# Attention: sums ahead of query halves, scaled diagonals on ScalarE, mask in the maximum

## The chip, the cores and the metric

The kernel runs on one core of a Trainium2 chip. The metric is the device time of one execution in microseconds. A core has five engines with a queue each, joined by semaphores: TensorE (PE; PEld is its weight load), VectorE (DVE), ScalarE (ACT), GpSimd (POOL) and SyncE (SP), which only issues transfers here. An engine takes its queue in order.

## The reference, cut to what matters

The kernel computes two transformer layers: linear attention and a mixture of experts, then causal attention and a feed-forward layer. The change touches the causal attention alone, here with B = 2 sequences of 1024 tokens and 16 heads:

```
qs  = concat([q_nope, rope(q_pe)])           # (b, h, s, 192), q = x @ wq
ks_ = concat([k_nope, rope(k_pe)])           # from a latent of 64
scores = einsum('bhqd,bhkd->bhqk', qs, ks_) * scale
scores = where(causal, scores, finfo.min)
attn = softmax(scores, axis=-1)
out = einsum('bhqk,bhkd->bhqd', attn, v)
```

## The kernel before

`phase_attention` runs once for each sequence. It goes through eight pairs of heads (`n`), and through ten steps (`x`) in each pair: a step is a block of 256 queries (`i`, 0 to 3) against a block of 256 keys (`jj` up to `i`). The steps that end a query block are x = 0, 2, 5 and 9 (`last_of`). The order on each engine is written out by hand, step by step.

**PE**, in step u: the score products of step u + 2 in two halves (`scores`, L1359, into one of two PSUM pairs), between and behind them what `aside` lists, then the value products of step u (`values`, L1382, into the bank `pv_ps`). `aside` lists in steps 0 to 3 one of the four query products of the next pair (`query`, L1327, all into the one bank `q_ps`), and in nearly all steps some pieces (`piece`, L1340): products of 128 queries with up to 512 keys, of which only the maximum of each row is wanted. There are 24 pieces to a pair, numbered 0 to 23, in two PSUM banks; 16 of them hold the causal diagonal, and for these a second matmul (L1343) adds -1e30 above it. In a middle pair steps 0 and 1 hold the pair's own last pieces, 21 to 23; steps 2 to 9 hold pieces 0 to 20 of the next pair. The maxima are subtracted from the scores by a last matmul of `scores` (L1365) with the matrix `minus`, four 128x128 diagonals to a query block.

**VectorE** does the rotary products of a query (`rope`, L1547 twice and L1550), the maxima of the pieces (`peaks`, L1555), behind the last piece of a block the diagonals (`spread`: L1564 joins the two halves of a row for blocks 2 and 3, L1568 writes the four diagonals), and reciprocals of the sums (`invert`, L1579). In steps 0 to 3 it takes the step's first piece ahead of the rotary products.

**ScalarE** does the exponentials (`probs`, L1441) and their rounding (`highs`, L1448) for step u + 2, in steps 0 to 3 the rounding of a query half (`q_high`, L1434, which waits for POOL's `rotate`), and at the end of a query block the copies of sums and products out of `pv_ps` (`sums`, L1459 and L1460). The first value product of the next block waits for them (`sums_sb`).

**POOL** completes the rotation (`rotate`, L1489), and computes the low halves of the queries (`q_low`, L1496), of the weights and of the exponentials (`low`, L1512), and the division's products (`product`, L1507).

A query thus goes: PE `query`, VectorE `rope`, POOL `rotate`, ScalarE `q_high`, POOL `q_low`; and since `q_ps` is one bank, query k + 1 waits for `rope` of query k.

## Time and profile before

| | us |
|---|---|
| median of three runs | 1459.39 (1458.5 to 1461.07) |
| the profiled execution | 1459.05 |
| its span, first to last instruction | 1457.2 |

| stretch, us | length | PE busy | DVE busy | ACT busy | POOL busy | granted clock |
|---|---|---|---|---|---|---|
| 500 to 890, attention of sequence 0 | 390 | 351.61 | 257.50 | 222.56 | 285.77 | 0.98 |
| 945 to 1333, attention of sequence 1 | 388 | 351.43 | 256.77 | 220.77 | 285.71 | 0.98 |
| the whole span | 1457.2 | 1227.6 | 844.7 | 626.2 | 961.9 | 0.93 |

The two attention stages are the same work twice. A matmul's record starts when it is issued and ends by a model of the pipeline, so neighbours overlap: the cost of one is read from the start of what follows. Where a row ends with a bracket, the engine was idle that long before it, and the name behind the arrow is what released it by the semaphores; where several semaphores are awaited, the view names the last to come by its inference, which can be another than the one that counted.

### The profile page before, as it was taken

The numbers are of one execution on the slowest core, as the hardware profiler recorded it, in microseconds if no ns is written. First come the engines' busy times: TensorE is split into PE (matmuls) and PEld (weight loads), VectorE is DVE, ScalarE is ACT, GpSimd is POOL, SyncE is SP. The second block draws the span as 40 slices with busy tenths as digits, with TensorE's granted clock in tenths as the row PEclk, the third lists the DMA queues.
The fourth block names the chain that finished last, engine by engine and source line by source line (L and its number), as shares of the span: only waits on it lengthen the run. The fifth ranks groups of instructions, "written<-read, shape, count | busy, mean of one in ns | idle before, by whom it ended". The sixth has DMA issues, their size and how long they took to land. (4 is left out here: it accounts for less than half of the span.)

```text
span 1457.2 us, 18876 instructions
## 1 busy us (share of the span) xinstructions
PE 1227.6 (84%) x5880; PEld 881.1 (60%) x5881; DVE 844.7 (58%) x1551; ACT 626.2 (43%) x1069; POOL 961.9 (66%) x700
## 2 busy tenths in 40 slices
PE   6974699999992489988998897689889998998797
PEld 5863455555551356666666666556666666666686
DVE  4578522222224667766676654767766776673567
ACT  3220233333320245565565564135655565565242
POOL 2025768888875457877788776557876787776454
PEclk9986799999995789999999998779999999999899
DMA  9348335555555000000000000000000000002001
GB/s 327 118 153 216 98 60 82 82 80 81 80 79 167 8 8 8 8 1 8 8 8 1 1 1 12 8 8 8 8 1 8 8 8 1 1 1 64 1 8 51
DMA packets 66509, 68.28 MB, mean 47 GB/s; under 512 B 15072, under 2 KB 59680, under 8 KB 66304
## 3 DMA queue, kind: packets, MB, share of 16 engines
q1 hardware_dynamic: 48336, 43.42, 10.0%
q0 software_dynamic: 15168, 20.72, 9.2%
q10 hardware_dynamic: 2928, 3.15, 0.7%
q8 instruction: 44, 0.72, 0.2%
q14 instruction: 33, 0.27, 0.1%
HBM read 46.17 MB, written 21.10 MB: 46 GB/s over the span
## 5 line engine op out<-in xcount | busy, mean ns | idle before, releaser
L1512 POOL TENSOR_TENSOR att_prob_lo<-att_prob,att_prob_hi 128x1024 fp32r<-128x1024 f32 (+1 forms) x160 | 346.7, 2167 | 114.1 <-ACT att_prob_hi L1448 114.0
L1555 DVE TENSOR_REDUCE att_peak<-all_bank 128x1 f32<-128x512 f32 (+3 forms) x384 | 207.4, 550 | 208.8 <-PE all_bank L1343 140.4
L1359 PE MATMUL all_bank<-att_q_hl,sequence_k_hl 128*128 128x512 f32 (+1 forms) x960 | 263.6, 385 | 0.0
L1382 PE MATMUL all_bank<-att_prob_hi,sequence_v_hl 128*128 128x512 f32 (+1 forms) x640 | 201.6, 396 | 35.3 <-POOL att_prob_lo L1512 19.1
L1441 ACT ACTIVATE att_prob<-all_bank 128x1024 f32<-128x1024 f32 (+1 forms) x160 | 150.6, 941 | 175.9 <-PE all_bank L1365 174.7
L1359 PEld LDWEIGHTS all_bank<-att_q_hl,sequence_k_hl 128*128 128x128 f32 x960 | 170.0, 192 | 26.1
L1340 PE MATMUL all_bank<-sequence_k_hl,att_q_hl 128*128 128x512 f32 (+3 forms) x384 | 171.0, 449 | 8.7 <-DVE att_peak L1555 8.3
L1448 ACT CAST att_prob_hi<-att_prob 128x1024 fp32r<-128x1024 f32 (+1 forms) x160 | 154.2, 964 | 5.1
L1327 PE MATMUL all_bank<-sequence_x_hl,sequence_w_hl 128*128 128x512 f32 x384 | 115.0, 438 | 46.3 <-DVE all_xT L1550 38.7
L1489 POOL TENSOR_TENSOR all_xT<-all_xT 128x512 f32<-128x512 f32 x64 | 82.4, 1288 | 106.1 <-DVE all_xT L1550 105.7
L916 PE MATMUL all_bank<-early_w_gu,moe_xgT 128*128 x316 | 148.9, 554 | 3.6 <-issue 2.4
L881 POOL DMA_INDIRECT sums<-moe_y,early_slot_far x79 | 125.5, 1589 | 36.0 <-issue 19.7
L1382 PEld LDWEIGHTS all_bank<-att_prob_hi,sequence_v_hl 128*128 128x128 f32 x640 | 108.0, 192 | 51.8 <-issue 24.7
L1579 DVE RECIPROCAL att_rden<-att_den 128x128 f32<-128x128 f32 x124 | 115.6, 939 | 26.8 <-POOL late_oT L1507 26.8
L1327 PEld LDWEIGHTS all_bank<-sequence_x_hl,sequence_w_hl 128*128 128x128 f32 x384 | 73.0, 201 | 77.2 <-DVE all_xT L1550 55.7
L1382 PE MATMUL all_bank<-att_prob_lo,sequence_v_hl 128*128 128x512 f32 x320 | 118.7, 371 | 0.0
L1365 PE MATMUL all_bank<-att_minus,all_bf 128*128 128x512 bf16 x320 | 117.6, 367 | 0.0
L1434 ACT CAST att_q_hl<-all_xT 128x512 fp32r<-128x512 f32 x64 | 39.7, 621 | 173.0 <-POOL all_xT L1489 173.0
L1008 DVE COPY moe_hidT<-all_bank 112x256 f32<-112x256 f32 x79 | 33.6, 425 | 123.4 <-PE all_bank L926 123.4
L1547 DVE TENSOR_TENSOR all_xT<-all_bank,sequence_cst_turned 32x512 f32<-32x512 f32 x128 | 88.8, 693 | 26.1 <-PE all_bank L1327 23.5
L871 POOL DMA_INDIRECT moe_xg<-x_rows,early_slot_row x79 | 84.2, 1065 | 26.1 <-issue 21.5
L935 PE MATMUL all_bank<-early_w_down,moe_hidT 112*128 x316 | 87.0, 398 | 12.1 <-issue 10.4
(244 smaller groups left out, 2103.6 us busy)
## 6 DMA issues: line engine op xcount, KB each, us to landing
sequence_w_raw<-wqk_rows SPq DMA_DIRECT2D x16, 256.0 KB, 2.7
early_w_gu<-in_gate SPq DMA_DIRECT2D x16, 224.0 KB, 5.7
early_w_gu<-in_up SPq DMA_DIRECT2D x16, 224.0 KB, 5.8
early_w_down<-in_down SPq DMA_DIRECT2D x1, 3584.0 KB, 19.8
sums<-early_zero SPq DMA_DIRECT2D x18, 128.0 KB, 3.7
all_xT<-in_xT SPq DMA_DIRECT2D x4, 512.0 KB, 7.6
all_x_tok<-in_x SPq DMA_DIRECT2D x1, 2048.0 KB, 16.3
x_rows<-all_x_tok SPq DMA_DIRECT2D x4, 512.0 KB, 3.0
```

The lines of the kernel that those rows point to most:

```text
L881: nc.gpsimd.indirect_dma_start(sums[s], bass.IndirectOffsetOnAxis(slot_far[:, r:r + 1], 0), y[:, s, :], None, bounds_check=last_far, compu ...
L916: mm = nc.tensor.matmul(gu_ps[s], xgT[:, s, k, :], w_gu[:, bass.ds(e * (KC * 2 * I) + k * 2 * I, 2 * I)], start=k == 0, stop=k == KC - 1)
L1327: mm = nc.tensor.matmul(q_ps, w_hl[:, ws, kc, h * P:(h + 1) * P], x_hl[:, xs, kc, c * WIDE:(c + 1) * WIDE], start=i == 0, stop=i == 3 * KC ...
L1340: mm = nc.tensor.matmul(ps[:, 0:w], q_hl[n % 2][:, 0, h, t * P:(t + 1) * P], k_hl[:, 0, k0:k0 + w], start=True, stop=not diagonal)
L1359: nc.tensor.matmul(ps, k_hl[:, ks, j * P:(j + 1) * P], q_hl[n % 2][:, qs, :, i * BW + q0:(i + 1) * BW], start=g == 0, stop=False)
L1365: mm = nc.tensor.matmul(ps, bf["ones"], minus[:, i, :].rearrange("p (h m) -> p h m", h=2)[:, :, q0:BW], start=False, stop=True)
L1382: mm = nc.tensor.matmul(out, v_hl[:, vs, j, :], part[:, u % 3, half * WIDE:half * WIDE + 2 * w].rearrange("p (h m) -> p h m", h=2), start= ...
L1441: nc.scalar.activation(prob[:, u % 2, 0:w], s_ps[u % 2][:, 0:w], ACT.Exp, scale=SCALE).then_inc(prob_sb, 1)
L1448: nc.scalar.copy(prob_hi[:, u % 3, 0:w], prob[:, u % 2, 0:w]).then_inc(hi_sb, 1)
L1512: nc.gpsimd.tensor_tensor(prob_lo[:, u % 3, 0:w], prob[:, u % 2, 0:w], prob_hi[:, u % 3, 0:w].bitcast(F32), ALU.subtract).then_inc(lo_sb, 1)
L1555: nc.vector.tensor_reduce(peak[:, n % 2, part, t // 2, h, t % 2:t % 2 + 1], piece_ps[y % 2][:, 0:w], AX_X, ALU.max).then_inc(peak_sb, 1)
L1579: nc.vector.reciprocal(rden[:, e % 2, cols], den[:, e % 2, cols]).then_inc(rden_sb, 1)
```

## The change

Four things in `phase_attention`, and the constants that they need.

- On ScalarE, `sums` stands ahead of `q_high` in a step. On POOL, `q_low` stands at the end of its own step, behind `low`, and no longer at the start of the next.
- The diagonals `minus` are made on ScalarE: `spread` is four activations of 128x128 (the identity, scaled by a row's maximum), at places given by `SPREAD_AT`: in step 4 for the next pair's block 0, in step 5 for block 1, in step 8 for block 2, in step 1 for the pair's own block 3. The sign moves into the stationary matrix (`less` holds -1).
- The matmul L1343 is gone. The maximum of a piece with the diagonal is one VectorE operation that adds the mask `late_wide` (in bf16; zeros, then the triangle), writes the sum back to the piece's bank and takes the maximum.
- The maximum of a row's second half starts from the first half's, so the join L1564 is gone.

```diff
@@ constants @@
-        bf = {n: bft[:, i, :] for i, n in enumerate(("ident", "ones", "late_q", "late_k"))}
+        bf = {n: bft[:, i, :] for i, n in enumerate(("ident", "less", "late_k"))}
+        bf["late_wide"] = bft[:, 4:8, :].rearrange("p a m -> p (a m)")
...
@@ the piece on PE @@
                     mm = nc.tensor.matmul(ps[:, 0:w], q_hl[n % 2][:, 0, h, t * P:(t + 1) * P],
-                                          k_hl[:, 0, k0:k0 + w], start=True, stop=not diagonal)
-                    if diagonal:
-                        mm = nc.tensor.matmul(ps[:, w - P:w], bf["late_q"], bf["ident"], start=False, stop=True)
+                                          k_hl[:, 0, k0:k0 + w], start=True, stop=True)
@@ ScalarE @@
+    SPREAD_AT = {4: [(1, 0)], 5: [(1, 1)], 8: [(1, 2)], 1: [(0, 3)]}
+                def spread(n, i):
+                    act.wait_ge(peak_sb, n * NP + block_needs[i])
+                    if n:
+                        act.wait_ge(s_mm, (n - 1) * NG + last_of[i] + 1)
+                    for a in range(4):
+                        done = nc.scalar.activation(minus[:, i, a * P:(a + 1) * P], bf["ident"], ACT.Copy,
+                                                    scale=peak[:, n % 2, 1, i, a // 2, a % 2:a % 2 + 1])
+                    done.then_inc(minus_sb, 1)
...
+                    if x in last_of:
+                        sums(n, last_of.index(x))
+                    for of, i in SPREAD_AT.get(x, ()):
+                        if 0 < n + of < PAIRS:
+                            spread(n + of, i)
+                    if n == 0 and x == 2:
+                        spread(0, NB - 1)
                     if made:
                         q_high(n + 1, x)
-                    if x in last_of:
-                        sums(n, last_of.index(x))
@@ POOL @@
-                        if 1 <= x <= QC:
-                            q_low(n + 1, x - 1)
...
+                    if n + 1 < PAIRS and x < QC:
+                        q_low(n + 1, x)
@@ VectorE @@
-                    nc.vector.tensor_reduce(peak[:, n % 2, part, t // 2, h, t % 2:t % 2 + 1], piece_ps[y % 2][:, 0:w],
-                                            AX_X, ALU.max).then_inc(peak_sb, 1)
-
-                def spread(n, i):
...
+                    half, whole = (peak[:, n % 2, a, t // 2, h, t % 2:t % 2 + 1] for a in range(2))
+                    if diagonal:
+                        if part:
+                            dve.wait_ge(peak_sb, n * NP + y - 1)
+                        nc.vector.tensor_tensor_reduce(ps, ps, bf["late_wide"][:, WIDE - w:WIDE], 1.0, half if part else MASKED,
+                                                       ALU.add, ALU.max, whole).then_inc(peak_sb, 1)
+                    else:
+                        nc.vector.tensor_reduce(half, ps, AX_X, ALU.max).then_inc(peak_sb, 1)
```

VectorE in steps 0 and 1 of a middle pair before (`all_xT` is the rotary's target, `att_peak` the maxima, `att_whole` and `att_minus` the join and the diagonals):

```order
L1550 TENSOR_TENSOR all_xT<-all_bank,sequence_cst_turned 128x512
L1555 TENSOR_REDUCE att_peak<-all_bank 128x1 x2
L1564 TENSOR_TENSOR att_whole<-att_peak 128x4
L1568 SCALAR_TENSOR_TENSOR att_minus<-all_bf,att_whole 128x512
L1547 TENSOR_TENSOR all_xT<-all_bank,sequence_cst_turned 32x512 x2
```

and now (each add-and-maximum is built as two ISA rows, the second of one column):

```order
L1567 TENSOR_TENSOR all_xT<-all_bank,sequence_cst_turned 128x512
L1577 ISA all_bank,att_peak<-all_bank,all_bf,att_peak 128x512
L1577 ISA att_peak 128x1
L1577 ISA all_bank,att_peak<-all_bank,all_bf,att_peak 128x512
L1577 ISA att_peak 128x1
L1564 TENSOR_TENSOR all_xT<-all_bank,sequence_cst_turned 32x512 x2
```

The join and the diagonals no longer stand between the last piece's maximum and the rotary products of the next query.

ScalarE in steps 0 and 1 of a middle pair before (`att_q_hl` is `q_high`, `att_den` and `late_oT` are the sums):

```order
L1448 CAST att_prob_hi<-att_prob 128x768
L1434 CAST att_q_hl<-all_xT 128x512
L1459 COPY att_den<-all_bank 64x256
L1460 COPY late_oT<-all_bank 64x256
L1459 COPY att_den<-all_bank 64x256
L1460 COPY late_oT<-all_bank 64x256
L1441 ACTIVATE att_prob<-all_bank 128x1024
L1448 CAST att_prob_hi<-att_prob 128x1024
L1434 CAST att_q_hl<-all_xT 128x512
```

and now:

```order
L1457 CAST att_prob_hi<-att_prob 128x768
L1468 COPY att_den<-all_bank 64x256
L1469 COPY late_oT<-all_bank 64x256
L1468 COPY att_den<-all_bank 64x256
L1469 COPY late_oT<-all_bank 64x256
L1433 CAST att_q_hl<-all_xT 128x512
L1450 ACTIVATE att_prob<-all_bank 128x1024
L1457 CAST att_prob_hi<-att_prob 128x1024
L1441 ACTIVATE att_minus<-all_bf,att_peak 128x128 x4
L1433 CAST att_q_hl<-all_xT 128x512
```

The sums have moved ahead of the query half, and four scaled copies stand in step 1 ahead of the next one.

## Rows read from the trace of the kernel before

**Rows 1.** busy us by stretch: length, PE, PEld, DVE, ACT, POOL, clock, DMA.

```profile
715.52:739.73 24.21, 20.18 (x97) 14.33 (x96) 15.05 (x24) 14.43 (x24) 17.60 (x12) 1.00 0.00 1
739.73:762.90 23.17, 23.15 (x118) 16.19 (x117) 17.61 (x28) 13.46 (x18) 18.48 (x12) 1.00 0.04 12
530.18:573.41 43.23, 40.21 (x197) 27.94 (x196) 34.81 (x52) 24.38 (x36) 32.90 (x21) 1.00 0.02 7
```

**Rows 2.** timeline, PE, one pair: start, us, instruction, [idle before <-releaser].

```profile
716.37 1.74 PE L1327 MATMUL all_bank<-sequence_x_hl,sequence_w_hl 128*128 128x512 f32 x6
...
721.85 1.65 PE L1327 MATMUL all_bank<-sequence_x_hl,sequence_w_hl 128*128 128x512 f32 x6 [0.58 <-DVE all_xT L1550]
...
725.55 0.70 PE L1382 MATMUL all_bank<-att_prob_hi,sequence_v_hl 128*128 128x512 f32 x2 [0.82 <-ACT late_oT L1460]
...
729.13 1.67 PE L1327 MATMUL all_bank<-sequence_x_hl,sequence_w_hl 128*128 128x512 f32 x6 [1.02 <-DVE all_xT L1550]
...
734.38 1.65 PE L1327 MATMUL all_bank<-sequence_x_hl,sequence_w_hl 128*128 128x512 f32 x6 [0.36 <-DVE all_xT L1550]
...
736.52 0.23 PE L1343 MATMUL all_bank<-all_bf 128*128 128x128 bf16 x1
738.02 0.71 PE L1382 MATMUL all_bank<-att_prob_hi,sequence_v_hl 128*128 128x512 f32 x2 [1.26 <-POOL att_prob_lo L1512]
...
763.78 1.74 PE L1327 MATMUL all_bank<-sequence_x_hl,sequence_w_hl 128*128 128x512 f32 x6
```

**Rows 3.** timeline, ScalarE of the same pair.

```profile
725.04 0.36 ACT L1460 COPY late_oT<-all_bank 64x256 f32<-64x256 f32 x1
...
737.51 0.36 ACT L1460 COPY late_oT<-all_bank 64x256 f32<-64x256 f32 x1
...
746.25 1.03 ACT L1441 ACTIVATE att_prob<-all_bank 128x1024 f32<-128x1024 f32 x1 [1.59 <-PE all_bank L1365]
```

**Rows 4.** timeline, VectorE of the same pair.

```profile
724.77 0.69 DVE L1555 TENSOR_REDUCE att_peak<-all_bank 128x1 f32<-128x512 f32 x1 [2.38 <-PE all_bank L1343]
725.50 0.71 DVE L1564 TENSOR_TENSOR att_whole<-att_peak 128x4 f32<-128x4 f32 x1
...
726.97 1.40 DVE L1547 TENSOR_TENSOR all_xT<-all_bank,sequence_cst_turned 32x512 f32<-32x512 f32 x2
...
738.52 0.69 DVE L1550 TENSOR_TENSOR all_xT<-all_bank,sequence_cst_turned 128x512 f32<-128x512 f32 x1
```

**Rows 5.** timeline, PE at two like spots, without and with L1343.

```profile
714.93 0.40 PE L1340 MATMUL all_bank<-sequence_k_hl,att_q_hl 128*128 128x512 f32 x1
...
715.40 0.28 PE L1382 MATMUL all_bank<-att_prob_lo,sequence_v_hl 128*128 128x256 f32 x1
...
719.46 0.40 PE L1340 MATMUL all_bank<-sequence_k_hl,att_q_hl 128*128 128x512 f32 x1
...
720.06 0.28 PE L1382 MATMUL all_bank<-att_prob_lo,sequence_v_hl 128*128 128x256 f32 x1
```

**Rows 6.** groups by shape, VectorE: busy us, mean ns | idle before.

```profile
L1555 DVE TENSOR_REDUCE att_peak<-all_bank 128x1 f32<-128x512 f32 x160 | 108.5, 688 | 116.8 <-PE all_bank L1340 62.3 <-PE all_bank L1343 52.3
...
L1929 DVE SCALAR_TENSOR_TENSOR ffn_hid<-all_bank,late_s_up,ffn_gated 128x512 f32<-128x512 f32 x20 | 14.9, 747 | 24.8 <-ACT ffn_gated L1886 15.4 <-POOL ffn_hid_hl L1903 9.2
...
L707 DVE TENSOR_TENSOR_SCAN route_ties_so_far<-route_ones,route_tie 128x256 f32<-128x256 f32 x1 | 0.7, 682 | 0.0
...
L806 DVE TENSOR_SCALAR route_far<-early_cst 128x1 f32<-128x1 f32 x1 | 0.1, 145 | 0.0
```

**Rows 7.** groups by shape, ScalarE.

```profile
L1886 ACT ACTIVATE ffn_gated<-all_bank,late_s_gate 128x512 f32<-128x512 f32 x20 | 13.8, 688 | 24.8 <-PE all_bank L1841 24.8
...
L649 ACT COPY early_z<-all_bank 128x128 f32<-128x128 f32 x16 | 3.5, 269 | 37.8 <-PE all_bank L608 37.8
```

**Rows 8.** timeline, step 8 of that pair, POOL, then PE.

```profile
752.73 2.39 POOL L1512 TENSOR_TENSOR att_prob_lo<-att_prob,att_prob_hi 128x1024 fp32r<-128x1024 f32 x1
...
757.57 0.62 PE L1382 MATMUL all_bank<-att_prob_hi,sequence_v_hl 128*128 128x512 f32 x2
```

More of the change, by code:

```diff
@@ L63, in const_columns @@
     for name, width in (("ident", P), ("cos", QT * ROPE), ("sin", QT * ROPE), ("before", P), ("iota", P), ("headmask", P),
-                        ("late_q", P), ("late_k", P), ("late_cols", 2 * P), ("row", 1)):
+                        ("late_q", P), ("late_k", P), ("late_cols", P), ("row", 1)):
         at[name] = (n, n + width)
@@ L96, in const_table @@
     put("late_k", np.where(f >= p, MASKED, 0.0))
-    q = np.arange(2 * P)[None, :] - P
-    put("late_cols", p == np.maximum(q + 1, 0))
+    put("late_cols", p == f + 1)
     put("row", p)
@@ L230, in _ @@
                 nc.gpsimd.memset(power[:], -0.5).then_inc(ones_sb, 1)
-                nc.gpsimd.memset(bf["ones"], 1.0)
+                nc.gpsimd.memset(bf["less"], -1.0)
                 pool.wait_ge(loaded_x, 32)
@@ L405, in _ @@
                 dve.wait_ge(loaded_cst, 32)
-                for name in ("ident", "late_q", "late_k", "late_cols"):
+                for name in ("ident", "late_k", "late_cols"):
                     nc.vector.tensor_copy(bf[name], cst[name])
+                nc.vector.memset(bf["late_wide"][:, 0:WIDE - P], 0.0)
+                nc.vector.tensor_copy(bf["late_wide"][:, WIDE - P:WIDE], cst["late_q"])
                 for n in range(B * KC):
@@ L1286, in phase_attention @@
         peak = m.sb("peak", [P, 2, 2, NB, 2, 2])
-        whole = m.sb("whole", [P, 2, NB, 2, 2])
         minus = m.sb("minus", [P, NB, WIDE], BF16)
@@ L1334, in piece @@
                     _, n, y = item
-                    t, h, _, k0, w, diagonal = pieces[y]
+                    t, h, _, k0, w, _ = pieces[y]
                     if n * NP + y >= 2:
@@ L1362, in scores @@
                         nc.tensor.matmul(ps[:, :, 0:P], bf["late_k"],
-                                         bf["late_cols"][:, P:2 * P].unsqueeze(1).to_broadcast([P, 2, P]),
+                                         bf["late_cols"].unsqueeze(1).to_broadcast([P, 2, P]),
                                          start=False, stop=False)
-                    mm = nc.tensor.matmul(ps, bf["ones"], minus[:, i, :].rearrange("p (h m) -> p h m", h=2)[:, :, q0:BW],
+                    mm = nc.tensor.matmul(ps, bf["less"], minus[:, i, :].rearrange("p (h m) -> p h m", h=2)[:, :, q0:BW],
                                           start=False, stop=True)
@@ L1464, in _ @@
                     q_high(0, k)
+                spread(0, 0)
+                spread(0, 1)
                 weights_high(1)
@@ L1467, in _ @@
                 highs(0)
+                spread(0, 2)
                 probs(1)
@@ L1552, in peaks @@
                 def peaks(n, y):
-                    t, h, part, _, w, _ = pieces[y]
+                    t, h, part, _, w, diagonal = pieces[y]
+                    half, whole = (peak[:, n % 2, a, t // 2, h, t % 2:t % 2 + 1] for a in range(2))
+                    ps = piece_ps[y % 2][:, 0:w]
                     dve.wait_ge(max_mm, n * NP + y + 1)
-                    nc.vector.tensor_reduce(peak[:, n % 2, part, t // 2, h, t % 2:t % 2 + 1], piece_ps[y % 2][:, 0:w],
-                                            AX_X, ALU.max).then_inc(peak_sb, 1)
-                def spread(n, i):
-                    top = peak[:, n % 2, 0, i]
-                    dve.wait_ge(peak_sb, n * NP + block_needs[i])
-                    if i >= NB // 2:
-                        top = whole[:, n % 2, i]
-                        nc.vector.tensor_tensor(top, peak[:, n % 2, 0, i], peak[:, n % 2, 1, i], ALU.max).then_inc(whole_sb, 1)
-                        dve.wait_ge(whole_sb, n * (NB // 2) + i - NB // 2 + 1)
-                    if n:
-                        dve.wait_ge(s_mm, (n - 1) * NG + last_of[i] + 1)
-                    nc.vector.scalar_tensor_tensor(minus[:, i, :].rearrange("p (a m) -> p a m", m=P),
-                                                   bf["ident"].unsqueeze(1).to_broadcast([P, 4, P]), -1.0,
-                                                   top.rearrange("p h t -> p (h t)").unsqueeze(2).to_broadcast([P, 4, P]),
-                                                   ALU.mult, ALU.mult).then_inc(minus_sb, 1)
+                    if diagonal:
[5 more added lines that the diff above has]
+                        nc.vector.tensor_reduce(half, ps, AX_X, ALU.max).then_inc(peak_sb, 1)
                 def invert(e, half):
@@ L1586, in beside @@
                         peaks(n, v)
-                        if v + 1 in block_needs:
-                            spread(n, block_needs.index(v + 1))
                 dve.wait_ge(turned_loaded, 16)
@@ L1948, in program @@
         cst = {n: cst_kept[:, a:z] for n, (a, z) in at.items() if z <= kept}
[L1949 to L1951 removed]
+        bft = m.sb("bf", [P, 8, P], BF16)
+        bf = {n: bft[:, i, :] for i, n in enumerate(("ident", "less", "late_k"))}
+        bf["late_cols"] = bft[:, 3:4, :].rearrange("p a m -> p (a m)")
+        bf["late_wide"] = bft[:, 4:8, :].rearrange("p a m -> p (a m)")
         power = m.sb("power", [P, NT])
```

6 lines of the change are left out of this document (2 added, 4 removed).

## Prediction

> **What bounds the kernel now.** I read the stage first, then the queues inside it. There are two attention stages, one per sequence, with eight head pairs each and ten steps to a pair. Pairs 1 to 6 repeat themselves: the query matmuls of one pair's step 0 start at 716.37 and those of the next at 763.78, 47.4 us later [rows 2]. So I take one pair apart and multiply by 12 (six in each sequence). 
>
> The waits of steps 1 to 3 are in the PE timeline [rows 2]. Three are queries waiting for the rotary product of the query before (0.58, 1.02 and 0.36 us), because one PSUM bank holds them all. Two are the first value product of a query block, at 725.55 (0.82) and 738.02 (1.26). Those wait for the sums of the block before. The ScalarE rows show it [rows 3]: the last copy of the sums ends at 725.04 + 0.36 = 725.40 and at 737.51 + 0.36 = 737.87, each 0.15 ahead of the matmul. The view names a POOL subtraction for the second; by the code that matmul needs only an earlier subtraction, so I put it to the copies. They are late because they stand behind `q_high`, which waits for POOL's rotation, though `pv_ps` was complete long before.
>
> **Part 1, sums ahead of `q_high`.** The four copies start as soon as `highs(u+2)` and the value products are done, some 3 us earlier in step 0 and 2 us in step 2. Both waits go. But what is late next is the rotary chain: query k+1 waits for VectorE's rotary of query k, which stands behind the maxima of a piece that PE issues after `scores(u+2, 1)`. A PE that reaches query 2 at 729.13 - 1.02 - 0.95 still needs the rotary to be done. So the step-1 wait is worth only what the chain gives back, which is part 2's business; the step-3 wait comes back in full, as nothing but `sums` and `low` holds the value product there. ScalarE now blocks on the value products in steps 0 and 2 ahead of `q_high`; `q_high` waits for the rotation anyway, which ends later. On POOL only a `product` in step 3 changes places with `q_low`, which nothing waits for.
>
> **Part 2, the diagonals leave VectorE.** In step 1 VectorE does the last piece's maximum (724.77), then `whole` (725.50) and the `minus` diagonals, and only then the rotary, at 726.97 [rows 4]. From 725.50 to 726.97 that is 1.47 us straight on the chain to query 2. Elsewhere the other three spreads stand where VectorE has room: nothing is gained.
>
> **Part 3, the mask moves from a matmul to the maximum.** The matmul L1343 (128 columns, 256 in all, 16 to a pair) costs its columns and a weight load that has nothing to hide behind. Two like spots show it [rows 5]: from a 512-wide piece to the start of the last of three 256-wide value matmuls it is 715.40 - 714.93 = 0.47 without it and 720.06 - 719.46 = 0.60 with it, so 0.13 us each.
> In its place 256 of the 384 maxima become an add-and-maximum that is two instructions: one over the columns that writes them back to PSUM, one that reads out a 128x1 result. The trace has no such pair, so I bound it [rows 6]. A 512-wide maximum is 688 ns and a two-input operation out of PSUM with a per-partition scalar 747; a 128x1 operation takes 145. Below nothing it can't be: the same columns pass, and an instruction is added. Low end 0 (the tail hidden), and at 512 columns high end 0.6, by the furthest row, the scan that carries a value from column to column: 682 ns for 256 columns, the rate of two passes. I take 0.16 (0.06 for the scalar, 0.10 of the tail), since a running maximum is what the reduction already does at full rate.
>
> **Part 4, the diagonals arrive on ScalarE.** Four 128x128 scaled copies to a spread. A 128x128 copy took 269 ns, a 128x512 activation with a per-partition scale 688, a quarter of it 172 [rows 7]; the 256-wide copies 360 [rows 3]. So 0.7 to 1.5 us a spread; I take 1.3, near the 128x128 row plus a pointer. That is 5.2 us a pair, on an engine busy 27.9 of 47.4 [rows 1]. The cover: step 1's runs while ScalarE would wait for the rotation, those of steps 4, 5 and 8 in gaps like the 1.59 us at 746.25 [rows 3]. The tightest place behind them is step 8's value product, whose subtraction ended at 752.73 + 2.39 = 755.12 with the matmul at 757.57 [rows 8], 2.45 us of margin. Two spreads (2.6) stand ahead of it on ScalarE, and PE comes sooner; the gaps swallow most, and I reckon 0.4 us left.
> A rule speaks against this part: the Trainium skill, ScalarE: Activation LUTs, Rules for kernel authors, says to do multiplications on VectorE, not ScalarE, VectorE being up to about three times faster. By the figures of that page of the Trainium skill (186 ns fixed, 93 for a pointer operand, 0.833 a column, neighbours overlapping by 93) a spread would be an estimated 1.2 us, against 0.69 for VectorE's one instruction. The rows agree on the price and not on the advice: ScalarE waits there, and VectorE holds the chain.
>
> **The sum for one pair**, step by step:
> - Query 2 before: 729.13. Less 0.13 (no L1343 ahead of the piece's maximum), plus 0.16, less 1.47: 727.69, a gain of 1.44. PE itself would be there about 727.05, so it still waits 0.6 for the rotary.
> - Query 3: again 0.13 less and 0.16 more: gain 1.41, at 732.97.
> - Step 3's value product: before, 738.02. Its piece and L1343 ended at 736.52 + 0.23 = 736.75, which is 2.37 after query 3; without the 0.13 it follows 2.24 after 732.97, at 735.21: gain 2.81. The copies it needs are done by about 734. With one more L1343 in that step, 2.94.
> - Steps 4 to 9: eleven L1343, 1.43. But VectorE's rotary of query 3 ended at 738.52 + 0.69, half a us ahead of step 4 [rows 4]; it now ends about 1.1 us behind its start, and the third piece of step 4 waits about 0.45 for a free bank. Left: 0.98.
> Together 3.9 us a pair, 47 us for twelve. The first pair of each sequence idles less (43.23 - 40.21 = 3.0 [rows 1]) and has the same 16 matmuls; I take 2.5 each, 5 in all. The last pair has two L1343: 0.5 for both. The opening ahead of the first pair loses three spreads on VectorE and pays sixteen maxima; I take 1 us each (0 to 2), 2 in all. The VectorE and POOL constants at the start cost nothing: VectorE waits for PE right after. Sum 54.5. The profiled run took 1459.05, so 1404.6; the median is 0.3 above it: **1405 us**.
>
> **Rivals.**
> *ScalarE becomes the bound.* If a scaled copy is 0.5 us rather than 0.33, a spread is 2.0, step 8's subtraction comes 1.4 later with 0.4 to spare: 1 us a pair lost in step 8 and about as much again in steps 4 to 6, where the sums stand behind a spread: 12 to 24 us back, 1417 to 1429. For it: an engine that goes from 59% to over 75% with queued waits. Against: the price would be past every row above. The rule of the Trainium skill named above points to this rival; its price is worked out from the rows.
> *The chain holds more than I think.* If PE merely waits elsewhere (pieces waiting for maxima in steps 4 to 9), the 1.43 of the matmuls does not come back and some of the 1.44 neither: 2 to 2.5 us a pair, 1425 to 1435. Against: VectorE was busy 17.6 of 23.2 in steps 4 to 9 and loses three spreads there.
> *Slower.* The add-and-maximum is so dear that VectorE sets steps 1 to 9. Two of them stand on the rotary chain and twelve behind it in steps 3 to 9, where VectorE has some 6 us free, about 0.5 each. Past 0.5 extra, every 0.1 costs 1.4 us a pair; the 3.9 are eaten at about 0.75 extra, and at 0.9 the kernel takes 1485. For it: it writes PSUM where the maximum wrote one column. Against: the two-input row of 747 ns runs at the rate of the reduction, and even the scan's rate would stay below 0.75.
> *Better than the sum.* Tail hidden, step 4 without a wait: 4.5 us a pair, about 1396.
>
> **How the numbers follow.** Forecast (1397 to 1414) 0.62; better 0.06; ScalarE bound 0.12; chain holds more 0.14; slower 0.03; and 0.03 for ending within 0.2%, about what a measurement can tell from no change. That gives faster 0.94, same 0.03, slower 0.03. The range leaves out the slow end and the farthest of the better: 1393 to 1428.
>
> **What would show it.** Right: a pair repeats at about 43.5 us; no wait of a value product on the sums in steps 1 and 3; queries 1 to 3 still waiting 0.5 to 0.8 us for the rotary; the 512-wide add-and-maximum with its tail at 0.8 to 0.9 us; four scaled copies in 1.3 us. Wrong: value products waiting for POOL's subtraction in steps 6 and 8 (ScalarE), or pieces waiting for maxima all through steps 4 to 9 (VectorE).

## The result

| | before | after |
|---|---|---|
| median, us | 1459.39 | 1401.61 (1399.83 to 1404.18, four runs) |
| profiled execution, us | 1459.05 | 1404.18 |
| its span, us | 1457.2 | 1402.4 |
| granted clock over the span | 0.93 | 0.93 |

The ratio is 0.9614, with an interval of 0.9596 to 0.9631: 57.8 us less. 1405 was predicted, in a range from 1393 to 1428. The profiled execution is the slowest of the four, so the spans differ by less than the medians.

Where the time went is told by the two attention stages, each taken from the first pair's first value products to the last pair's last. Together they took 718.15 us before and take 667.88 now: 50.3 of the 54.8 us by which the spans differ. The remaining 4.5 us lie in the rest of the program, where only the openings ahead of the first pairs and the constants changed. In the kernels below this rest varies from 728 to 739 us, so small edits are judged by the stages ("stages" in the table of experiments).

### The profile page after: what moved, and what is told of

It reads as the page before. It is cut to its first block and busy times, and to the rows that moved or that the text cites. A ratio compares the mean times of both kernels' runs of the same rounds, so it can differ in the third digit from the quotient of the medians.

```text
span 1402.4 us, 18855 instructions
## 1 busy us (share of the span) xinstructions
PE 1188.5 (85%) x5570; PEld 877.9 (63%) x5625; DVE 789.7 (56%) x1712; ACT 697.6 (50%) x1325; POOL 956.0 (68%) x700
## 5 line engine op out<-in xcount | busy, mean ns | idle before, releaser
L1358 PE MATMUL all_bank<-att_q_hl,sequence_k_hl 128*128 128x512 f32 (+1 forms) x960 | 257.1, 378 | 0.0
L1381 PE MATMUL all_bank<-att_prob_hi,sequence_v_hl 128*128 128x512 f32 (+1 forms) x640 | 190.4, 379 | 16.8 <-ACT late_oT L1469 15.3
L1328 PE MATMUL all_bank<-sequence_x_hl,sequence_w_hl 128*128 128x512 f32 x384 | 115.1, 438 | 48.1 <-DVE all_xT L1567 40.5
L1381 PEld LDWEIGHTS all_bank<-att_prob_hi,sequence_v_hl 128*128 128x128 f32 x640 | 112.7, 189 | 41.0 <-issue 22.1
L1580 DVE TENSOR_REDUCE att_peak<-all_bank 128x1 f32<-128x512 f32 (+1 forms) x128 | 83.7, 657 | 74.1 <-PE all_bank L1341 69.9
L1577 DVE CUSTOM_DVE_ANT_0 all_bank<-all_bank,all_bf,att_peak 128x256 f32<-128x256 f32 (+2 forms) x128 | 75.6, 591 | 75.9 <-PE all_bank L1341 73.9
L1564 DVE TENSOR_TENSOR all_xT<-all_bank,sequence_cst_turned 32x512 f32<-32x512 f32 x128 | 88.8, 693 | 26.4 <-PE all_bank L1328 23.8
L1577 DVE CUSTOM_DVE_ANT_0 all_bank<-all_bank,all_bf 128x128 f32<-128x128 f32 (+3 forms) x128 | 63.0, 499 | 60.9 <-PE all_bank L1341 60.3
```

The costliest lines, as they stand in the source:

```text
L1328: mm = nc.tensor.matmul(q_ps, w_hl[:, ws, kc, h * P:(h + 1) * P], x_hl[:, xs, kc, c * WIDE:(c + 1) * WIDE], start=i == 0, stop=i == 3 * KC ...
L1358: nc.tensor.matmul(ps, k_hl[:, ks, j * P:(j + 1) * P], q_hl[n % 2][:, qs, :, i * BW + q0:(i + 1) * BW], start=g == 0, stop=False)
L1381: mm = nc.tensor.matmul(out, v_hl[:, vs, j, :], part[:, u % 3, half * WIDE:half * WIDE + 2 * w].rearrange("p (h m) -> p h m", h=2), start= ...
L1564: nc.vector.tensor_tensor(swapped[o:o + 32, c % 2], q_ps[i:i + 32], sin[i:i + 32, cols], ALU.mult)
L1577: nc.vector.tensor_tensor_reduce(ps, ps, bf["late_wide"][:, WIDE - w:WIDE], 1.0, half if part else MASKED, ALU.add, ALU.max, whole).then_i ...
```

## The profile after

Stretches of one middle pair, steps 0 to 3 and steps 4 to 9, and of the first pair: length, then busy us of PE, PEld, DVE, ACT and POOL, granted clock, DMA share, GB/s. They answer [rows 1].

```profile
700.68:722.07 21.39, 19.03 (x92) 14.19 (x91) 12.74 (x23) 15.05 (x28) 16.22 (x11) 1.00 0.00 1
722.07:744.46 22.39, 21.86 (x106) 16.46 (x106) 16.88 (x39) 17.25 (x31) 19.50 (x13) 1.00 0.05 13
529.52:569.24 39.72, 37.25 (x177) 27.78 (x178) 29.17 (x64) 28.68 (x52) 32.30 (x21) 1.00 0.03 8
```

The clock is 1.00 in all three, as before. Steps 0 to 3 became 2.8 us shorter, steps 4 to 9 only 0.8, and in those TensorE now idles 0.53 us. The PE timeline of the pair shows each wait, as [rows 2] did:

```profile
701.65 1.74 PE L1328 MATMUL all_bank<-sequence_x_hl,sequence_w_hl 128*128 128x512 f32 x6
707.13 1.66 PE L1328 MATMUL all_bank<-sequence_x_hl,sequence_w_hl 128*128 128x512 f32 x6 [0.95 <-DVE all_xT L1567]
712.98 1.64 PE L1328 MATMUL all_bank<-sequence_x_hl,sequence_w_hl 128*128 128x512 f32 x6 [0.72 <-DVE all_xT L1567]
718.17 1.64 PE L1328 MATMUL all_bank<-sequence_x_hl,sequence_w_hl 128*128 128x512 f32 x6 [0.43 <-DVE all_xT L1567]
720.71 0.71 PE L1381 MATMUL all_bank<-att_prob_hi,sequence_v_hl 128*128 128x512 f32 x2 [0.26 <-ACT late_oT L1469]
732.38 0.69 PE L1381 MATMUL all_bank<-att_prob_hi,sequence_v_hl 128*128 128x512 f32 x2 [0.53 <-ACT late_oT L1469]
...
745.43 1.74 PE L1328 MATMUL all_bank<-sequence_x_hl,sequence_w_hl 128*128 128x512 f32 x6
```

From query 0 to query 0 it is 43.78 us (47.41 before). Three queries still wait for the rotary product. The 0.95 of the first holds a matmul whose record is missing, L1364 ahead of the query: in the six middle pairs that have the record the wait is 0.72, and the step is as long. Of the value products, step 1's no longer waits, step 3's waits 0.26 instead of 1.26, and step 6's waits 0.53 where the view of before has no bracket (what that hides is told under "L1343" below). ScalarE of the same pair shows why:

```profile
719.06 0.37 ACT L1468 COPY att_den<-all_bank 64x256 f32<-64x256 f32 x1 [1.40 <-DVE att_rden L1588]
...
720.20 0.36 ACT L1469 COPY late_oT<-all_bank 64x256 f32<-64x256 f32 x1
...
726.93 1.27 ACT L1441 ACTIVATE att_minus<-all_bf,att_peak 128x128 bf16<-128x128 bf16 x4
...
730.74 0.37 ACT L1468 COPY att_den<-all_bank 64x256 f32<-64x256 f32 x1
...
731.87 0.36 ACT L1469 COPY late_oT<-all_bank 64x256 f32<-64x256 f32 x1
732.26 1.28 ACT L1441 ACTIVATE att_minus<-all_bf,att_peak 128x128 bf16<-128x128 bf16 x4
```

In step 2 the sums, now ahead of `q_high`, wait 1.40 us for VectorE's reciprocals of the block two before, whose `den` buffer they take, and end at 720.56, 0.15 ahead of the value product. In step 5 they stand behind the scaled copies of step 4 and all that those pushed back, and end at 732.23, again 0.15 ahead of the value product.

VectorE on the chain to query 2 (compare [rows 4]), with no join and no diagonals between maximum and rotary:

```profile
709.97 0.76 DVE L1577 CUSTOM_DVE_ANT_0 all_bank<-all_bank,all_bf,att_peak 128x512 f32<-128x512 f32 x1 [2.17 <-PE all_bank L1341]
710.64 0.14 DVE L1577 DVE_READ_ACCUMULATOR2_ANT att_peak<- 128x1 f32 x1
710.82 1.40 DVE L1564 TENSOR_TENSOR all_xT<-all_bank,sequence_cst_turned 32x512 f32<-32x512 f32 x2
```

Groups by shape, busy us and mean ns of one, the new operations on ScalarE and VectorE (compare [rows 6, 7]):

```profile
L1441 ACT ACTIVATE att_minus<-all_bf,att_peak 128x128 bf16<-128x128 bf16 x256 | 81.6, 390 | 9.7 <-DVE att_peak L1577 9.4
...
L1577 DVE DVE_READ_ACCUMULATOR2_ANT att_peak<- 128x1 f32 x256 | 36.3, 142 | 0.0
...
L1577 DVE CUSTOM_DVE_ANT_0 all_bank<-all_bank,all_bf,att_peak 128x512 f32<-128x512 f32 x32 | 24.2, 755 | 33.6 <-PE all_bank L1341 33.3
L1577 DVE CUSTOM_DVE_ANT_0 all_bank<-all_bank,all_bf 128x512 f32<-128x512 f32 x32 | 22.3, 702 | 12.3 <-PE all_bank L1341 12.3
```

## Experiments

Steps are those of a middle pair, from the last value product of one to that of the next, in us; "pair" is the sum of all ten. A ratio is taken against runs of the kernel before made beside the kernel's own (p1 and p2 ran twice, the others four to ten times). What other steps do is told where it matters.

| kernel | median | ratio to before | stages | step 1 | 2 | 3 | 6 | pair |
|---|---|---|---|---|---|---|---|---|
| before | 1459.39 | | 718.15 | 6.74 | 5.90 | 6.81 | 3.99 | 47.4 |
| a1_sums | 1457.59 | 0.9984 [0.9959, 1.0009] | 719.82 | 5.73 | 8.46 | 5.73 | 4.01 | 47.9 |
| a2_diag | 1451.39 | 0.9952 [0.9932, 0.9972] | 710.93 | 6.72 | 5.13 | 6.81 | 3.99 | 46.6 |
| a3_mask | 1436.12 | 0.9859 [0.9826, 0.9891] | 695.30 | 6.84 | 5.61 | 6.75 | 4.00 | 45.8 |
| after | 1401.61 | 0.9614 [0.9596, 0.9631] | 667.88 | 5.72 | 5.49 | 5.65 | 4.30 | 43.8 |
| u1_sums_behind | 1417.91 | 0.9712 [0.9679, 0.9745] | 682.69 | 6.85 | 4.51 | 6.76 | 4.00 | 44.7 |
| u2_diag_dve | 1431.02 | 0.9810 [0.9794, 0.9827] | 693.73 | 5.73 | 6.76 or 8.33 | 5.65 | 4.04 | 45.3 or 46.6 |
| u3_mask_pe | 1434.46 | 0.9828 [0.9812, 0.9845] | 695.20 | 5.75 | 6.13 | 5.72 | 3.99 | 45.6 |
| u4_q_low_later | 1418.38 | 0.9723 [0.9707, 0.9740] | 681.41 | 5.73 | 6.23 | 5.66 | 4.61 | 44.9 |
| p1_max_twice | 1443.94 | 0.9896 [0.9871, 0.9922] | 700.53 | 5.75 | 6.36 | 6.06 | 3.53 | 46.1 |
| p2_copies_twice | 1430.09 | 0.9801 [0.9782, 0.9821] | 692.48 | 5.71 | 5.50 | 5.66 | 5.47 | 45.0 |
| i1_rope_first | 1358.92 | 0.9323 [0.9300, 0.9345] | 626.80 | 4.75 | 4.51 | 4.54 | 4.06 | 40.5 |
| i2_late_copies | 1398.74 | 0.9604 [0.9584, 0.9625] | 665.64 | 5.72 | 5.49 | 5.65 | 3.99 | 43.5 |
| i3_both | 1358.29 | 0.9347 [0.9303, 0.9391] | 628.33 | 4.75 | 4.51 | 4.54 | 3.99 | 40.4 |

### One part alone, in the kernel before

a2_diag and a3_mask keep the changed kernel's place of `q_low` on POOL; that move was not run by itself. In step 1 of the traces `q_low` starts right behind `low` with either order.

**a1_sums**: the sums ahead of `q_high`.

```diff
+                    if x in last_of:
+                        sums(n, last_of.index(x))
                     if made:
                         q_high(n + 1, x)
-                    if x in last_of:
-                        sums(n, last_of.index(x))
```

> The kernel before with the block sums ahead of the query half on ScalarE, nothing else. My theory (the rotary chain holds the queries of steps 1 to 3): the wait in step 1 goes, but query 2 still starts when the rotary of query 1 is done, so only the step-3 wait of 1.26 us comes back: 1.2 us a pair, and somewhat more in the first pair, 15 to 20 us, 1440 to 1445 us. Rival (each recorded wait of TensorE is worth its length): 0.82 + 1.26 = 2.1 us in 14 pairs, 29 us, 1430 us.

Nothing came of it: 1457.59, and the stages are 1.7 us longer. Steps 1 and 3 gained 1.0 and 1.1 us, and step 2 lost 2.6. Its PE rows of queries 2, first of the same pair, then of the last middle pair of sequence 1:

```profile
729.85 2.71 PE L1327 MATMUL all_bank<-sequence_x_hl,sequence_w_hl 128*128 128x512 f32 x6 [2.06 <-DVE all_xT L1550]
...
1271.01 1.65 PE L1327 MATMUL all_bank<-sequence_x_hl,sequence_w_hl 128*128 128x512 f32 x6 [2.08 <-DVE all_xT L1550]
```

TensorE came to query 2 earlier, but the rotary did not, so the waits of steps 1 and 2 became one of 2.06 us. What follows it differs. The same kernel's stretches, the wait and the 5 us behind it, the last middle pair first (columns as above):

```profile
1268.93:1271.01 2.08, 0.00 (x0) 0.00 (x1) 2.05 (x4) 0.00 (x0) 0.00 (x0) 1.00 0.00 0
1271.01:1276.01 5.00, 4.82 (x23) 3.35 (x23) 3.02 (x5) 2.70 (x3) 4.89 (x3) 1.00 0.00 0
727.79:729.85 2.06, 0.00 (x0) 0.00 (x0) 2.03 (x4) 0.00 (x0) 0.00 (x0) 1.00 0.00 0
729.85:734.85 5.00, 5.00 (x17) 3.65 (x18) 1.46 (x3) 1.44 (x2) 4.85 (x3) 0.66 0.00 0
```

Behind the second wait the granted clock is 0.66 over 5 us, part of them at the lower level of 1.2 GHz, and 17 matmuls pass where 23 passed at 1.00. Step 2 takes 8.46 us with the fall and 6.91 without: the fall costs 1.55 us, in eleven of twelve middle pairs. The one pair without it takes 46.29 us, 1.1 less than before: that much of the waits did come back.

**a2_diag**: the diagonals on ScalarE; the mask stays a matmul, the join is eight 128x1 maxima to a pair, and the sums stay behind `q_high`. Against the changed kernel (with `sums` moved back as well):

```diff
+                    if diagonal:
+                        mm = nc.tensor.matmul(ps[:, w - P:w], bf["late_wide"][:, WIDE - P:WIDE], bf["ident"], start=False,
+                                              stop=True)
...
-                        nc.vector.tensor_tensor_reduce(ps, ps, bf["late_wide"][:, WIDE - w:WIDE], 1.0, half if part else MASKED,
-                                                       ALU.add, ALU.max, whole).then_inc(peak_sb, 1)
...
+                        nc.vector.tensor_reduce(later[:, y % 2:y % 2 + 1], ps, AX_X, ALU.max).then_inc(later_sb, 1)
+                        dve.wait_ge(later_sb, n * NP // 3 + part_of[y] + 1)
+                        nc.vector.tensor_tensor(whole, half, later[:, y % 2:y % 2 + 1], ALU.max).then_inc(peak_sb, 1)
```

> The kernel before with the diagonals as scaled copies on ScalarE; the mask stays a matmul, the sums stay behind the query half, and the join of the two halves is eight 128x1 maxima a pair on VectorE. My theory: the rotary of query 1 starts about 1.25 us earlier, but the value product of step 1 still waits for the sums, so TensorE reaches query 2 only about 1.1 us earlier: 13 to 16 us, 1443 to 1447 us. Rival (a busy-time view: VectorE is not the bound, and ScalarE gets 5 us a pair more): no gain, 1459 us or more.

1451.39, less than I expected. Only step 2 gained, 0.77 us, about the 0.69 of the diagonals; steps 1 and 3 wait for the sums as before. And the join, now of one column, still costs as much as with four. Its VectorE row, then the POOL row beside it:

```profile
718.49 0.72 DVE L1586 TENSOR_TENSOR att_peak<-att_peak,att_later 128x1 f32<-128x1 f32 x1
```

```profile
717.92 1.27 POOL L1518 TENSOR_TENSOR att_q_hl<-all_xT,att_q_hl 128x512 fp32r<-128x512 f32 x1
```

POOL's `q_low` ends at 719.19 and the join at 719.21. u4_q_low_later, below, tests this.

**a3_mask**: the mask in the maximum, without join; the diagonals stay one VectorE operation (as in u2_diag_dve, next), the sums behind `q_high`.

> The kernel before with the mask added where the maximum is taken (so the join falls away); diagonals in one VectorE instruction, sums behind the query half. My theory: 0.13 us for each of eleven matmuls in steps 4 to 9, and 0.7 us in step 1 as the join leaves the rotary chain: 2 us a pair, 25 to 30 us, 1430 to 1435 us. Rival (VectorE's dearer maxima eat it): 1445 us or more. If the parts only add, this, the two runs before it and the kernel after must sum: the three gains together 58 us.

1436.12, close above my expectation. Steps 4 to 9 are those of the changed kernel but for step 6, and steps 1 and 3 wait for the sums as before. The three parts alone give -1.7, 7.2 and 22.9 us of the stages, 28.4 together; all at once give 50.3. That they don't add has two causes in these rows: what the sums free is lost again at the rotary (and at the clock) while join and diagonals stand there, and what the other two free at the rotary lies in part behind the wait for the sums (in u1_sums_behind, next section, query 2 has no wait left).

### One part undone, in the changed kernel

**u1_sums_behind**: the sums behind `q_high` and behind the copies of their step.

> The changed kernel with the sums behind the query half again. My theory: step 1 loses little, since query 2 waits for the rotary anyway; step 3 loses about 1.3 us a pair: 1417 to 1421 us. Rival (recorded waits count in full): 2.1 us a pair, 1431 us.

1417.91: steps 1 and 3 cost 1.1 us more each, step 2 costs 1.0 less, as the wait for the sums covers the one for the rotary; step 6 gains 0.3. That is 14.8 us of the stages, where in the kernel before the same edit gave nothing.

**u2_diag_dve**: the diagonals as one VectorE operation again, with no join.

```diff
-                    for of, i in SPREAD_AT.get(x, ()):
-                        if 0 < n + of < PAIRS:
-                            spread(n + of, i)
...
                         peaks(n, v)
+                        if v + 1 in block_needs:
+                            spread(n, block_needs.index(v + 1))
```

> The changed kernel with the diagonals back on VectorE (one instruction of 0.7 to 1.1 us, no join). My theory: the rotary of query 1 is 0.75 us later, and query 2 with it; ScalarE loses 5 us a pair of work, so the wait of 0.53 us that the value product of step 6 now has for the sums goes. Net 0 to 0.4 us a pair, 1402 to 1408 us. Rival (the diagonals were worth their 1.47 us): 1418 us or more.

1431.02, more than I expected and on the rival's side, but not for its reason. VectorE, then POOL, then PE, in steps 1 and 4 of one pair:

```profile
670.55 1.22 DVE L1569 SCALAR_TENSOR_TENSOR att_minus<-all_bf,att_peak 128x512 bf16<-128x512 bf16 x1
...
686.92 2.10 DVE L1569 SCALAR_TENSOR_TENSOR att_minus<-all_bf,att_peak 128x512 bf16<-128x512 bf16 x1
```

```profile
669.93 1.29 POOL L1495 TENSOR_TENSOR att_q_hl<-all_xT,att_q_hl 128x512 fp32r<-128x512 f32 x1
...
686.62 1.84 POOL L1511 TENSOR_TENSOR att_prob_lo<-att_prob,att_prob_hi 128x768 fp32r<-128x768 f32 x1
```

```profile
673.96 2.08 PE L1328 MATMUL all_bank<-sequence_x_hl,sequence_w_hl 128*128 128x512 f32 x6 [1.98 <-DVE all_xT L1549]
```

The diagonals, 0.69 us in [rows 4]'s pair (726.25 to 726.94, between two rows shown there), took 1.22 and 2.10 here. They end 0.55 us after the POOL operation does (671.77 against 671.22; 689.02 against 688.46). Query 2 then waits 1.98 to 2.00 us in every middle pair, and in six of twelve the clock falls as in a1_sums: step 2 takes 8.33 instead of 6.76.

**u4_q_low_later**: u2_diag_dve, with POOL's `q_low` behind the next step's `rotate`, away from the diagonals of step 1.

```diff
                         if x < QC:
                             rotate(n + 1, x)
+                        if 1 <= x <= QC:
+                            q_low(n + 1, x - 1)
                     if u + AHEAD < STEPS:
                         low(u + AHEAD)
-                    if n + 1 < PAIRS and x < QC:
-                        q_low(n + 1, x)
```

> The changed kernel with the diagonals on VectorE (as in the run u2_diag_dve, 1431.02 us), and with POOL's q_low of a step placed behind the rotate of the next step instead of at the end of its own. Theory: the diagonals read two tensors from SBUF, and such a VectorE operation waits until the POOL operation that runs beside it is over; in step 1 that is q_low, and 0.53 us of the 1.22 us are this wait. With q_low gone from there the diagonals of step 1 take 0.69 us, query 2 waits 1.45 us instead of 1.98, TensorE's clock stays at 1.00 and step 2 takes about 6.2 us in every pair instead of 6.76 or 8.33: 1413 to 1423 us. Rival: the 1.22 us are the operation's own, for what stands ahead of it on VectorE; then the wait stays near 2 us and the time at 1428 to 1434.

1418.38, as the theory had it. VectorE and PE at the same spots, and PE in step 6:

```profile
670.91 0.69 DVE L1569 SCALAR_TENSOR_TENSOR att_minus<-all_bf,att_peak 128x512 bf16<-128x512 bf16 x1
```

```profile
673.80 1.65 PE L1328 MATMUL all_bank<-sequence_x_hl,sequence_w_hl 128*128 128x512 f32 x6 [1.46 <-DVE all_xT L1549]
...
693.50 0.73 PE L1381 MATMUL all_bank<-att_prob_hi,sequence_v_hl 128*128 128x512 f32 x2 [0.79 <-POOL att_prob_lo L1511]
```

With `q_low` elsewhere the diagonals of step 1 take 0.69 us in all twelve middle pairs, the wait is 1.46, and step 2 takes 6.23 us in all twelve pairs, without a fall of the clock. POOL's later `low` costs 0.6 in step 6. Diagonals on VectorE still cost 13.5 us of the stages here, against 25.9 in u2_diag_dve.

**u3_mask_pe**: the mask as a matmul again, plain maxima and 128x1 joins (the diff of a2_diag), the rest as changed.

> The changed kernel with the mask back as a matmul, plain maxima, and the join as eight 128x1 maxima a pair on VectorE. My theory: 0.13 us for each of the eleven matmuls of steps 4 to 9, 0.1 to 0.3 on the rotary chain: 1.6 us a pair and the same in the first pair, 1422 to 1427 us. Rival (the masked maxima cost on VectorE what the matmuls saved): 1402 us.

1434.46: more than I expected. Steps 4 to 9 take 23.3 us as before, and the join of step 1 takes 0.72 us again, beside `q_low`, so step 2 takes 6.13 instead of 5.49. In a middle pair steps 4 to 9 cost 0.9 us more than in the changed kernel and step 2 0.64 more; the pair costs 1.8 (1.6 expected), and a first pair 2.9, not 1.6. Of the 32.9 us between the medians, 27.3 lie in the stages; the rest of the program varies as said above.

### Work doubled

**p1_max_twice**: every add-and-maximum made twice, on the same columns. **p2_copies_twice**: every four scaled copies made a second time, into a spare tile. Nothing is left out.

```diff
+                        nc.vector.tensor_tensor_reduce(ps, ps, bf["late_wide"][:, WIDE - w:WIDE], 1.0, half if part else MASKED,
+                                                       ALU.add, ALU.max, whole).then_inc(again_sb, 1)
...
```

> The changed kernel with each add-and-maximum done twice in a row, so it costs 0.5 to 0.9 us more. By the prediction's slower rival (room of about 0.5 each on VectorE, then 1.4 us a pair for every 0.1): 1440 to 1480 us, near the kernel before. Rival (VectorE has room, only the two on the rotary chain count): 1415 to 1422 us.

1443.94, inside my range: 32.7 us more in the stages. The rotary chain takes 0.9 us of it in step 2 and 0.4 in step 3, and pieces wait for their maxima in steps 4 and 5 (4.76 and 4.36 us, instead of 3.70 and 3.66). The second operation costs 0.40 to 0.82 us, by width, from start to start (0.64 on the mean), and the kernel is still 15 us below the one before: VectorE is the place where a dearer maximum decides, as the slower rival had it, but the point at which it turns the change seems to lie above the 0.75 us that I worked out.

```diff
+                    for a in range(4):
+                        first = nc.scalar.activation(spare[:, a * P:(a + 1) * P], bf["ident"], ACT.Copy,
+                                                     scale=peak[:, n % 2, 1, i, a // 2, a % 2:a % 2 + 1])
...
```

> The changed kernel with the four scaled copies of a spread done a second time into a spare tile, 1.2 us more on ScalarE at each of the four places. If ScalarE already sets step 6 (its sums stand behind the spread of step 4), step 6 loses the whole 1.2 us, and step 8 or 9 may lose more: 1417 to 1432 us. If ScalarE has room: 1402 us.

1430.09. In middle pairs nearly all of it lies in step 6, whose value product now waits 1.71 us for the sums instead of 0.53; steps 1 to 3 and 8 do not move. The first and last pairs lose 2.8 and 2.7 us each, the last in step 3's sums.

### What the waits left are worth

**i1_rope_first**: VectorE takes the rotary products ahead of the step's first piece, in the order in which TensorE issues them.

```diff
-                    if items and items[0][0] == "query":
-                        items[0:2] = items[1::-1]
```

> The changed kernel with VectorE's rotary products ahead of the step's first piece in steps 0 to 3. If the chain query, piece, maximum, rotary, next query is what still holds steps 1 to 3, the three query waits (0.95, 0.72 and 0.43 us) go: up to 2.1 us a pair, 1372 to 1388 us. If the pieces' banks or ScalarE take over, about 1400 us.

1358.92, better than I expected, 42.7 us below the changed kernel's median. VectorE in step 0, first in the changed kernel (query 0 starts at 701.65), then here (689.59):

```profile
704.25 0.69 DVE L1580 TENSOR_REDUCE att_peak<-all_bank 128x1 f32<-128x512 f32 x1 [2.91 <-PE all_bank L1341]
704.97 1.40 DVE L1564 TENSOR_TENSOR all_xT<-all_bank,sequence_cst_turned 32x512 f32<-32x512 f32 x2
```

```profile
691.37 1.40 DVE L1564 TENSOR_TENSOR all_xT<-all_bank,sequence_cst_turned 32x512 f32<-32x512 f32 x2 [2.09 <-PE all_bank L1328]
```

In the changed kernel VectorE idles 2.91 us for a piece that TensorE issues after the query, and turns to the query 3.32 us after its start; here it waits for the query itself, and starts 1.78 us after it. Two stretches of this kernel, steps 0 to 3 and 4 to 9 of the pair:

```profile
688.62:706.94 18.32, 18.32 (x91) 14.21 (x91) 12.56 (x22) 14.98 (x28) 16.45 (x11) 1.00 0.00 1
706.94:729.09 22.15, 21.87 (x106) 16.45 (x107) 16.55 (x40) 17.24 (x31) 19.24 (x13) 1.00 0.05 13
```

TensorE is busy throughout steps 0 to 3: no query waits, and no value product. Step 6 still waits 0.28 us for the sums. This version beats both kernels. It gained more than the waits that I had added up, because a bracket is less than what a wait costs: steps 1 to 3 are 3.1 us shorter, and their brackets come to 2.1 (0.72, 0.72, 0.43 and 0.26). Step 2 alone went from 5.49 to 4.51 us by one bracket of 0.72. A bracket counts from the modelled end of the matmul before, which lies behind the point at which the next one would have started: in the changed kernel the query at 701.65 starts 0.03 us after an L1364 whose record is 0.38 us long.

**i2_late_copies**: the copies one or two steps later. **i3_both**: with i1_rope_first.

```diff
-    SPREAD_AT = {4: [(1, 0)], 5: [(1, 1)], 8: [(1, 2)], 1: [(0, 3)]}
+    SPREAD_AT = {6: [(1, 0)], 7: [(1, 1)], 9: [(1, 2)], 1: [(0, 3)]}
```

> The changed kernel with the scaled copies of steps 4, 5 and 8 moved to steps 6, 7 and 9, behind the sums of step 5. If the step-6 wait of 0.53 us comes from ScalarE's copies ahead of the sums, it goes: 0.5 us a pair, 1394 to 1398 us. If it comes from elsewhere (the reciprocals): 1402 us.

> Both of the edits before together: if the two waits are independent, their gains add, 1366 to 1382 us; if the rotary order only moves the wait onto ScalarE, no better than the first of the two.

1398.74, just above my range: step 6 got back 0.3 us and still waits 0.21, and the last pair lost 1.1 (32.77 against 31.64; its step 1 now waits 0.81 us for the sums). With the rotary first nothing is left of it: 1358.29 can't be told from 1358.92.

## Why the prediction was right, step by step

- **What bounds the kernel.** Right in the main: the waits of steps 1 to 3 and the columns of L1343. That steps 4 to 9 give time back only by columns was wrong in step 6 (see L1343). i1_rope_first shows how far the first part went: without rotary waits TensorE idles nowhere in steps 0 to 3.
- **Query 2 and query 3.** Measured from query 0, query 2 came 12.76 us later before and comes 11.33 now, a gain of 1.43 (predicted 1.44); query 3 gained 1.49 (1.41). The wait that was to remain is 0.72 (predicted 0.6).
- **The 1.47 us of join and diagonals.** Right in size, wrong in what it was made of. The join is not 0.71 us of VectorE work but a wait for POOL, and with the join gone the diagonals wait in its place (u2_diag_dve). So the join's half of part 2 could hardly be had alone: a2_diag, with the diagonals alone gone, gained 0.77 us in step 2, and a3_mask, with the join gone and the diagonals kept, 0.29. "Elsewhere nothing is gained" fits the kernel before, which idles 0.02 us in steps 4 to 9, but not the changed one: with the diagonals back on VectorE, those of step 4 take up to 2.10 us, a piece waits for its maximum, and step 5 takes 4.1 us instead of 3.66 (u2_diag_dve; a3_mask does not show it).
- **Part 1, worth what the chain gives back.** Right: in a1_sums the step-1 wait came back at query 2, and only the pair without a fall of the clock kept what step 3 gained (1.1 us). That the longer wait could pull the clock down was not in the prediction.
- **Step 3's value product.** The gain is 2.59, not 2.81: it still waits 0.26 us for the sums, which I had done by about 734 in the time of before. I let them wait for the value products; they wait for a reciprocal on VectorE (1.40 us, in the rows above).
- **Add-and-maximum.** On the chain it is 710.82 - 709.97 = 0.85 us to the next operation against 0.73 [rows 4]; 0.12 more, 0.16 taken. Its two parts are 755 and 142 ns, and overlap.
- **L1343.** Steps 4, 5, 7, 8 and 9 took 19.32 us and take 18.08 now: 1.24 for nine, 0.138 each (0.13 predicted). The two of step 6 gave nothing back, and the sum had counted them. The value product of step 6 was released by the sums in the kernel before too, under a bracket too short to be shown; ScalarE's last copy and that product in the pair of [rows 2]:

```profile
749.53 0.36 ACT L1460 COPY late_oT<-all_bank 64x256 f32<-64x256 f32 x1
```

```profile
750.04 0.70 PE L1382 MATMUL all_bank<-att_prob_hi,sequence_v_hl 128*128 128x512 f32 x2
```

The copy ends at 749.89, and the product starts 0.15 behind it, as the products behind the copies of [rows 3] do. Without these matmuls step 6 takes 3.99 us as before, where no new copies stand ahead of its sums (a3_mask, i2_late_copies); where it waits for nothing it takes 3.53 (p1_max_twice). Steps 4 to 9 together gained 0.9 us (0.98 predicted), but with another loss in them than the one that I named, which comes next.
- **Step 4 waits 0.45 for a bank.** Wrong: no wait. The maximum that frees the third piece's bank is the one of the step's first piece:

```profile
724.11 0.41 DVE L1577 CUSTOM_DVE_ANT_0 all_bank<-all_bank,all_bf 128x256 f32<-128x256 f32 x1
724.43 0.14 DVE L1577 DVE_READ_ACCUMULATOR2_ANT att_peak<- 128x1 f32 x1
```

```profile
725.14 0.33 PE L1341 MATMUL all_bank<-sequence_k_hl,att_q_hl 128*128 128x384 f32 x1
```

It was read out at 724.57, 0.57 us ahead of the piece. The time went in step 6 instead.
- **Scaled copies.** 1.27 us for four (1.3 predicted). The estimate of 1.2 by the figures of the Trainium skill, ScalarE: Activation LUTs, agrees with it. The tightest place was not step 8's subtraction, which has 1.5 us left and not 0.4, but step 6's sums: the copies lengthen that step by 0.33 us, which i2_late_copies gets back, and in middle pairs p2_copies_twice moves that place alone. It is the place that the ScalarE rival named for steps 4 to 6, at a third of its price. On VectorE the four products cost 25.9 us of the stages more (u2_diag_dve), or 13.5 with `q_low` out of their way (u4_q_low_later). So the rule of the Trainium skill, ScalarE: Activation LUTs, Rules for kernel authors, to do multiplications on VectorE does not pay here, as the prediction weighed it.
- **The sum.** Predicted against measured, in us less: twelve middle pairs 47 and 43.4; first pairs 5 and 7.0; last pairs 0.5 and -0.1; everything else 2 and 4.5. The total, 54.5 against 54.8 between the spans, is closer than its terms, and that was luck: 3.6 us too much in the middle pairs (0.3 each: 0.2 in steps 0 to 3, where step 3 still waits for the sums, and 0.1 in steps 4 to 9) was made good by 2.0 in the first ones and by the rest of the program. In that rest the openings are 2.6 us shorter (2 predicted), and the tail behind attention, the same work in both, took 2.8 us less at a higher granted clock. Before, then after:

```profile
1332.66:1457.20 124.54, 102.98 (x611) 89.09 (x609) 75.57 (x152) 44.06 (x69) 65.39 (x59) 0.89 0.12 36
```

```profile
1280.63:1402.40 121.77, 100.32 (x611) 86.57 (x609) 75.49 (x152) 44.01 (x69) 65.33 (x59) 0.93 0.12 37
```

Why the clock is higher there is open; the change does not touch the tail, which takes 120.3 to 124.6 us in the other kernels.

## What to carry to other kernels

Ask of every step between a releaser and the one who waits whether it is work or itself a wait: here a join of four columns was priced as 0.71 us of VectorE, and most of it was a wait for POOL. Parts of a change that lie on one chain are not worth their sum: alone they gave 28 us, together 50. And where an engine waits for a product that another one has had ready, look at the order in that one's queue first: swapping two entries there was worth 42.7 us in the changed kernel, against 57.8 for the whole change (in the kernel before it was not run). And an engine with no bracket may still have been released late: compare the start with the end of what it waits for.

## What the runs showed of the hardware

**VectorE waits for POOL.** Two operations here read two tensors from SBUF, the diagonals and the join. In the trace of before the 44 diagonals that start with no POOL operation running take 692 ns on the mean, and the 20 that start beside one take 1594; the join takes 163 ns (two of them) and 702 (thirty). Next to POOL the diagonals end 0.55 us after it does, and all thirty joins 0.02 us after it. [rows 4] has one: the join ends at 726.21. POOL in that trace:

```profile
724.92 1.27 POOL L1496 TENSOR_TENSOR att_q_hl<-all_xT,att_q_hl 128x512 fp32r<-128x512 f32 x1
```

It ends at 726.19. POOL is held up in turn: in u2_diag_dve a `q_low` behind the stretched diagonals took 1.73 us instead of 1.29. The Trainium skill, SBUF — State Buffer, "Who interferes with whom", states it: a VectorE instruction with two SBUF inputs contends with a GpSimd instruction that reads SBUF, and the one that comes second is blocked, not slowed. The trace agrees, and the add-and-maximum, which reads one of its two tensors from PSUM, does not wait: 512 wide and with a pointer, in the changed kernel, 14 that start with no POOL operation running take 750 ns on the mean, and 18 that start beside one 759.

**TensorE's clock after one wait.** After waits of 1.98 to 2.10 us the granted clock fell in 17 of 24 cases (a1_sums, u2_diag_dve), to 0.66 over the 5 us behind the wait and so in part to its lower level, and that cost some 1.55 us each time; after waits of 1.46 (u4), 1.61 (p1) and 1.71 us (p2) step times show no fall in any middle pair. What decides among the 24 is open: the wait with no fall in a1_sums, of 2.08 us, is as long as the others. The Trainium skill, TensorE: Matmul & The Clock Gate, "A second HAM failure mode: psum-queue depth-cycling", tells of idling between groups of matmuls that cycle through PSUM banks, which makes the clock swing between its two levels; there the idling comes again and again, and here the fall follows one wait of some 2 us in a pair, for a single bank.
